# Gated cross-attention layer: rows of x on partitions, probabilities turned by DMA

## The reference, cut to what matters

```python
Sim = (h @ w1)[:, :, None] + (ctx @ w2)[:, None, :] + einsum('bid,bjd->bij', h * w3, ctx) + b_sim[0]   # h = layernorm(x)
A = softmax(Sim, axis=2)
hq_hat = einsum('bij,bjd->bid', A, ctx)
Batt = softmax(max(Sim, axis=2), axis=1)
hc_hat = broadcast(einsum('bi,bid->bd', Batt, h))
x = x + tanh(g_xattn) * (concatenate([h, hq_hat, h * hq_hat, h * hc_hat]) @ W_qv + b_qv)
x = x + tanh(g_ffn) * ffn(layernorm(x))      # router, top 2 of 8 experts, capacity 1280 (not touched)
```

## Time and profile before

| | us |
|---|---|
| three runs, median | 2335.67 |
| lowest and highest of the three | 2333.89, 2336.94 |
| the profiled execution's own time | 2335.5 |
| its span | 2333.8 |
| PE busy | 2220.5 (95%) |
| DVE busy | 1631.7 (70%) |
| ACT busy | 1139.5 (49%) |
| mean granted clock of PE | 0.985 |

### The profile page before, as it was taken

How to read it: one execution, slowest core, us unless ns; L and a number is a source line. 1 busy time by engine, 2 the same in 40 slices (tenths; PEclk the granted TensorE clock), 3 DMA queues, 4 the chain that set the end, 5 groups by cost and what they waited for, 6 DMA issues and landing times.

```text
span 2333.8 us, 46974 instructions
## 1 busy us (share of the span) xinstructions
PE 2220.5 (95%) x16817; PEld 1607.4 (69%) x16817; DVE 1631.7 (70%) x3445; ACT 1139.5 (49%) x1607; POOL 144.6 (6%) x143
## 2 busy tenths in 40 slices
PE   5899999999999999999879998599999999999997
PEld 4788888888888888888634544456564655656463
DVE  7688888888888888887856678546554555646450
ACT  6565555544555554555633334336362534546260
POOL 0000000000000000000002222101101010100101
PEclk9999999999999999999999999799999999999999
DMA  7811110011111001101355553333435333333411
GB/s 211 251 28 47 45 45 27 18 45 45 45 45 45 18 27 45 45 27 43 148 200 199 213 184 119 103 104 86 109 124 135 113 99 103 90 103 90 132 61 22
DMA packets 164944, 212.31 MB, mean 91 GB/s; under 512 B 106148, under 2 KB 106276, under 8 KB 156700
## 3 DMA queue, kind: packets, MB, share of 16 engines
q1 hardware_dynamic: 154012, 191.13, 24.9%
q0 software_dynamic: 10880, 20.52, 4.5%
HBM read 123.66 MB, written 71.52 MB: 84 GB/s over the span
## 4 chain that ended last, share of the span: by engine, by line
PE 75%; DVE 13%; ACT 4%; issue 4%; DMA 1%; DVEq 1%; ACTq 0%; POOL 0%; another core or an unknown queue 0%; SPq 0%; POOLq 0%
PE ps L1275 20%; PE ps L1951 18%; PE ps L1966 18%; PE ps L1288 12%; PE ps L1701 5%; DVE arena L828 1%; DVE arena L727 1%; DVE arena L725 1%; ACT arena L1150 1%; DVE arena L822 1%; DVE arena L750 1%; DVE arena L815 1%; DVE arena L734 1%; ACT arena L1147 1%; DVE arena L1530 0%
## 5 line engine op out<-in xcount | busy, mean ns | idle before, releaser
L1275 PE MATMUL ps<-arena 128*128 128x256 f16 x4800 | 555.8, 274 | 25.1 <-DMA arena<-arena 9.9
L1288 PE MATMUL ps<-arena 128*128 (+1 forms) x4864 | 561.0, 273 | 7.3 <-DVE arena L822 7.3
L1275 PEld LDWEIGHTS ps<-arena 128*128 128x128 f16 x4800 | 470.1, 98 | 89.4 <-issue 16.6
L1288 PEld LDWEIGHTS ps<-arena 128*128 128x128 f16 x4864 | 475.2, 98 | 68.0 <-DVE arena L822 7.0
L1951 PE MATMUL ps<-arena 128*128 128x320 f16 x3072 | 421.0, 300 | 17.7 <-DMA arena<-rows 17.7
L1966 PE MATMUL ps<-arena 128*128 128x512 f16 x1920 | 415.7, 379 | 0.0
L1951 PEld LDWEIGHTS ps<-arena 128*128 128x128 f16 x3072 | 301.5, 98 | 136.9 <-issue 17.7
L1966 PEld LDWEIGHTS ps<-arena 128*128 128x128 f16 x1920 | 187.9, 98 | 225.2
L1137 ACT ACTIVATE arena<-ps,arena (+1 forms) x192 | 148.9, 775 | 282.8 <-PE ps L1275 282.8
L1701 PE MATMUL ps<-arena 128*128 128x512 f16 x1080 | 240.4, 380 | 10.6 <-DMA arena<-feats 10.6
L1875 DVE SCALAR_TENSOR_TENSOR arena<-arena 128x640 f16<-128x640 f32 x128 | 113.0, 883 | 136.1 <-ACT arena L1919 136.1
(11 more groups left out here) (249 smaller groups left out, 1821.7 us busy)
## 6 DMA issues: line engine op xcount, KB each, us to landing
arena<-in_L_ffn_w SPq DMA_DIRECT2D x64, 1024.0 KB, 10.0
arena<-feats SPq DMA_DIRECT2D x16, 1536.0 KB
arena<-in_x SPq DMA_DIRECT2D x32, 512.0 KB, 3.9
feats<-arena SPq DMA_DIRECT2D x16, 1024.0 KB, 3.9
rows<-arena SPq DMA_DIRECT2D x1, 10320.0 KB, 32.0
feats<-arena SPq DMA_DIRECT2D x16, 512.0 KB, 3.5
out<-arena SPq DMA_DIRECT2D x16, 512.0 KB, 2.8
arena<-in_L_xattn_W_qv SPq DMA_DIRECT2D x4, 1024.0 KB, 9.6
```

Source lines behind the costliest of these rows:

```text
L1275: mm = pe.matmul(out, ctxT[:, 2 * t + h, s, k, :], query[:, r, k, :], start=(k == 0 and s + r == 0), stop=(k == KD - 1 and s == 1))
L1288: mm = pe.matmul(acc[k], ctxN[:, 2 * t + h, s, k * P:(k + 1) * P], prob[:, bass.ds(a % 3, 1), r, h, :].rearrange("p o i -> p (o i)"), star ...
```

## The change

Scores now have the rows of x on partitions. The unit of work is 128 rows (`U` = 32 units, two halves of a block), and ctx is taken in 7 chunks (`NC`) of four tiles, 512 columns (`TC`, `CW`), of which the last has 130 columns. The queries are the stationary operand and `ctxT`, laid out with ctx rows on the free axis, is the moving one. A row's maximum is then a reduction along the free axis: it goes into the exponential's bias, and the row sum into its accumulator. The last tile's two rows are ordinary columns. The probabilities come out with rows of x on partitions and are turned for the second product by a DMA transpose for each chunk (`turn_p`), from two staging buffers into one buffer for each chunk. In half i of block b (u = 2b + i), PE does the scores of unit u and the products of unit u-2, chunk by chunk, while ACT and DVE do the softmax of unit u-1.

The queries are formed from rows by DVE and turned by DMA (`turn_q`): those of an odd unit in the first half of SP's body, those of the next block's even unit in its second half. The features are stored as rows, and the merge loads them by one DMA transpose for each block (`load_feats`); its order is changed, and the rows of x have a load of their own (`load_x`). In the prologue tiles 0 to 7 are turned by PE and tiles 8 to 25 by DMA, one transpose for each; group scales come from sums of squares in place of sizes, over four tiles; scores of unit 1 follow those of unit 0 by three chunks. The pooled row is accumulated along partitions and summed by PE once at the end. The table of blank rows is written in pieces through the loop. The core of the diff (functions that go with it are left out where there is "..."):

```diff
--- before.py
+++ after.py
-    def load_block(self, sp, x, feats, b, v):
-        rows = bass.ds(b * 256, 256)
-        sp.dma_start(self.ft[v].rearrange("p f s k i -> p (f s k i)"),
-                     feats[bass.ds(b, 1)].rearrange("o p f c -> (o p) (f c)")).then_inc(self.f_loaded[v], 16)
-        sp.dma_start(self.x2[v], x[rows, :].rearrange("(q p) d -> p q d", p=P)).then_inc(self.x_loaded[v], 16)
+    def load_feats(self, sp, feats, b, v):
+        sp.dma_start_transpose(self.ft[v].rearrange("p f s k i -> p (f s k) i"),
+                               feats[bass.ds(b * 256, 256)].rearrange("i f s d -> i (f s d)"))\
+            .then_inc(self.f_loaded[v], 16)
+
+    def load_x(self, sp, x, b, v):
+        sp.dma_start(self.x2[v], x[bass.ds(b * 256, 256), :].rearrange("(q p) d -> p q d", p=P))\
+            .then_inc(self.x_loaded[v], 16)
...
     IB = 256
     NB = NI // IB
     QT = IB // P
+    U = NI // P
     JT = -(-J // P)
-    NP = JT // 2
     FT = mg.FT
     JR = J - (JT - 1) * P
-    AHEAD = 5
-    BY_PE = 4
-    SLOTS = NP + AHEAD
-    assert JT == 2 * NP
+    TC = 4
+    CW = TC * P
+    NC = -(-J // CW)
+    TILES = [(TC * c, min(TC * c + TC, JT)) for c in range(NC)]
+    COLS = [(CW * c, min(CW * c + CW, J)) for c in range(NC)]
+    NPAIR = JT // 2
+    LAST = NC - 1
+    LAG = 3
+    XR = 4
+    BLANKS = 3
+    BY_PE = list(range(2 * TC))
+    assert TILES[LAST][1] - TILES[LAST][0] == 2 and JT == 2 * NPAIR
...
+    UNIT0 = LAG + 2 * (LAST - LAG) + 1
...
+        def turn_ctx(j):
+            sp.wait_ge(c_lo, j // 2 + 1)
+            sp.dma_start_transpose(ctxT[:, :, j * P:(j + 1) * P], ctxN[:, j].rearrange("p s d -> p (s d)"))\
+                .then_inc(ct_turned[j // TC], 16)
+
+        def turn_q(u, q):
+            sp.wait_ge(row_step, RK * (u + 1))
+            apart(sp, sp_passed)
+            sp.wait_ge(qk_done, UNIT0 if isinstance(u, int) and u == 2 else NC * (u - 1))
+            apart(sp, sp_passed)
+            sp.dma_start_transpose(qT[:, q], qh[:, q].rearrange("p s d -> p (s d)")).then_inc(q_turned[q], 16)
+
+        def turn_p(u, c):
+            sp.wait_ge(p_ready, NC * u + c + 1)
+            apart(sp, sp_passed)
+            if not isinstance(u, int) or u:
+                sp.wait_ge(av_done, NC * (u - 1) + c + 1)
+                apart(sp, sp_passed)
+            if c < LAST:
+                sp.dma_start_transpose(PT[:, c], stage[:, c % 2].rearrange("p s j -> p (s j)"))\
+                    .then_inc(pt_turned[c], 16)
+            else:
+                sp.dma_start_transpose(PTl, stl.rearrange("p n j -> p (n j)")).then_inc(pt_turned[c], 16)
...
+        def body(b, first=False, last=False, norms=True, loads=True, piece=None):
+            u = 2 * b
+            for c in range(NC):
+                turn_p(u - 1, c)
+                if c == 1 and not first and not last:
+                    turn_q(u + 1, 1)
+                if c == 3 and loads:
+                    if not first:
+                        sp.wait_ge(acc_step, 2 * (u - 2))
+                        apart(sp, sp_passed)
+                    load_x(b + 2)
+                if c == 4 and not first:
+                    store_f(u - 3, 1)
+                if c == 5 and norms:
+                    store_e(b + 1)
+            if piece is not None:
+                blank_rows(*piece)
+            for c in range(NC):
+                if not last:
+                    turn_p(u, c)
+                if c == 4:
+                    store_f(u - 2, 0)
+                if c == 5 and norms:
+                    turn_q(u + 2, 0)
...
+        for c in range(2, NC):
+            for j in range(*TILES[c]):
+                if j not in BY_PE:
+                    turn_ctx(j)
...
+        turn_q(2, 0)
+        for c in range(NC):
+            turn_p(0, c)
...
+        sp.wait_ge(qk_done, NC * U)
         mg.load_weights(sp)
+        body(NB, last=True, norms=False, loads=False)
...
+        def low(u, par, c):
+
+            dve.wait_ge(hi_done, NC * u + c + 1)
+            p = slot(par, c)
+            if c < LAST:
+                dve.scalar_tensor_tensor(out=stage[:, c % 2, 1, :], in0=p, scalar=pscale[:, c:c + 1],
+                                         in1=stage[:, c % 2, 0, :], op0=ALU.mult, op1=ALU.subtract)\
+                   .then_inc(p_ready, 1)
...
+        def half(b, i, first=False, last=False, norms=True):
+
+
+            u = 2 * b + i
+            par, old = i, 1 - i
+            ob = b if i else b - 1
+            for c in range(NC):
+                if not last:
+                    chunk_max(NC * u + c, par, c)
+                if not (last and i):
+                    low(u - 1, old, c)
+                if c == 0 and not (last and i):
+                    pool_top(u - 1, ob, old)
+                if c == 1 and not (first and not i):
+                    outputs(u - 3, b - 1 if i else b + XR - 2, old)
+                if c == 2:
+                    if not (first and not i):
+                        output_lows(u - 3, old)
+                    if not (last and i):
+                        pool_rows(u - 1, ob, old)
...
+        def probabilities(u, par, c):
+
+            p = slot(par, c)
+            if c == 0:
+                act.wait_ge(m_step, MK * (u + 1))
+                if not isinstance(u, int) or u >= 2:
+                    act.wait_ge(l_step, 2 * u - 2)
+            act.activation(p, p, ACT.Exp, bias=neg[:, par:par + 1], accum_out=ls[:, par, c:c + 1])\
+               .then_inc(exp_done, 1)
+            if c < LAST:
+                if c >= 2:
+                    act.wait_ge(pt_turned[c - 2], 16 * (u + 1))
+                elif not isinstance(u, int) or u:
+                    act.wait_ge(pt_turned[c + 4], 16 * u)
+            elif not isinstance(u, int) or u:
+                act.wait_ge(pt_turned[c], 16 * u)
+            act.wait_ge(exp_done, NC * u + c + 1)
+            if c < LAST:
+                act.activation(stage[:, c % 2, 0, :], p, ACT.Identity, bias=zero[:, 0:1], scale=pscale[:, c:c + 1])\
+                   .then_inc(hi_done, 1)
...
+        def half(b, i, first=False, last=False, norms=True):
+            u = 2 * b + i
+            par, old = i, 1 - i
+            for c in range(NC):
+                if not last:
+                    scores(NC * u + c, c % 4, par, c, NC * (u - 2) + c + 1)
+                if not (last and i):
+                    probabilities(u - 1, old, c)
+                if c == 1 and not (last and i):
+                    pool_weight(u - 1)
+                if c == 2 and not (first and not i):
+                    output_highs(u - 3, old)
...
+        def scores(bank, q, c):
+            a, z = COLS[c]
+            out = psS[bank][:, 0:z - a]
+            for k in range(KD):
+                for s, r in ((0, 0), (0, 1), (1, 0)):
+                    mm = pe.matmul(out, qT[:, q, s * KD + k, :], ctxT[:, r * KD + k, a:z],
+                                   start=(k == 0 and s + r == 0), stop=(k == KD - 1 and s == 1))
+            mm.then_inc(qk_done, 1)
+
+        def products(u, q, c, first=False):
+
+            pe.wait_ge(pt_turned[c], 16 * (u + 1))
+            if c == 0 and not first:
+                pe.wait_ge(acc_step, 2 * u - 3)
+            a, z = TILES[c]
+            for j in range(a, z):
+                if j == JT - 1:
+                    mm = pe.matmul(psO[q], PTl[:, 2, :], ctxN[:, j, 0, :], start=False, stop=True)
+                    continue
+                for s, r in ((0, 0), (0, 1), (1, 0)):
+                    turned = PT[:, c, s * TC + j - a, :] if c < LAST else PTl[:, s, :]
+                    mm = pe.matmul(psO[q], turned, ctxN[:, j, r, :], start=(j + s + r == 0), stop=False)
+            mm.then_inc(av_done, 1)
+
+        def half(b, i, first=False, last=False):
+            u = 2 * b + i
+            for c in range(NC):
+                if not last:
+                    if c == 0:
+                        pe.wait_ge(q_turned[i], 16 * b)
+                    pe.wait_ge(scores_ready, NC * u + c - 1)
+                    scores(c % 4, i, c)
+                if first and not i and c == LAST:
+                    pe.wait_ge(c_tail, 1)
+                products(u - 2, i, c, first)
...
         with sp.Fori(0, NB // 2 - 1) as n:
             for v in range(2):
+                sp.wait_ge(y_done, QT * (2 * n + v + 1))
+                apart(sp, sp_passed)
+                mg.load_feats(sp, feats, 2 * n + v + 2, v)
                 store(2 * n + v, v, n)
                 sp.wait_ge(y_step, YK * (2 * n + v + 1))
                 apart(sp, sp_passed)
-                sp.wait_ge(y_done, QT * (2 * n + v + 1))
-                mg.load_block(sp, x, feats, 2 * n + v + 2, v)
+                mg.load_x(sp, x, 2 * n + v + 2, v)
```

More of the change, by code:

```diff
@@ L706, in query_rows @@
+            s.wait()
+            s.step(dve.tensor_scalar(ew[:, bass.ds(b * QT, QT)], ewt, 1 / LN_SCALE, bs[:, 0:1], ALU.mult, ALU.add))
+        def query_rows(u, b, q, row, at):
```

(91 more changed lines are left out.)

1150 lines of the change are left out of this document (414 added, 736 removed).

## The result

The changed kernel takes 2383.69 us (median of 4 runs, 2381.66 to 2384.46), the kernel before 2336.31 us (2333.89 to 2337.44) on the same chip. The ratio is 1.0203, 95% interval 1.0185 to 1.0221: slower by 2.0%. The profiled execution has a span of 2382.6 us against 2333.8, and a mean granted clock of 0.967 against 0.985.

The account below looks back on a forecast made before the run. It took PE's streaming to bound the attention half. Loop +36, prologue +5, drain +3 and merge -6 made +38 us on 2335.5 us: 2373 us, range 2325 to 2412.

Parts of the forecast that it names:

- Rival A: Attention loop: PE waits for the queries' transpose in each block, then runs at half clock; 2373 us; chance 0.52.
- B: Attention loop: PE waits for the queries, but the clock stays up; 22 us less, 2351 us; chance 0.14.
- C: Attention loop: queries land in time, nothing waits, the shorter block's full 54 us is kept; 2284 us; chance 0.15.
- D: Merge: a features' transpose takes over 17.1 us and each block waits; at 20 us, 41 more, about 2414; chance 0.11.
- The wait, 4.8 us: Attention loop, block boundary: PE stands still until the next block's queries are turned by DMA, 4.8 us (3.3 to 6.0).
- The half clock, 1.6 us: Attention loop, behind each wait for queries: PE returns at half clock, costing another 1.6 us (1.3 to 2.0, lower end 0).
- a clock that stays up through the gap: Attention loop: sign that would make the prediction wrong; it expected granted clock 0.50 for some 3 us behind each gap.
- The block without waits, 65.2 us: Attention loop: if PE never waited, a block of 256 rows would go from 68.8 to 65.2 us.
- The prologue, +5: Before the attention loop: single-tile transposes and ACT's order put PE's first steady half at about 93 us; +5 us (-7 to +15).
- The drain, +3: Between loop and first merge: weights queued ahead of transposes, pooled weight late, 47 us against 44; +3 us (-5 to +12).
- The merge, -6: Merge and route: features' load issued before the store shortens PE's early wait, steady part unchanged; -6 us (-10 to +3).
- The DMA share of the merge, 0.92: Merge: with features loaded by transposes, the DMA share goes from 0.58 to 0.92 within blocks of 17.1 us.

Follow-up runs that it names:

- 18 filler matmuls: Changed kernel plus 18 matmuls that nothing needs, put on PE ahead of its wait for the queries in each block: 2353.67 us.
- the kernel with the earlier turn: Changed kernel with the transpose of the next block's even queries issued after the probabilities of chunk 4 instead of chunk 5: 2290.72 us.
- The later sums: Changed kernel with PE's prologue sums for the group after next taken behind the present group's scores instead of ahead of them: 2374.07 us.

## Why the prediction was right, and where its terms were off

**Direction and main term.** Forecast 2373 us, slower; measured 2383.69. The span grew by 48.8 us where +38 was forecast; of the 10.8 between them the prologue is 9.7, the loop 1.2 and the drain 1.0, and merge and experts take 1.0 back. Rival A, the wait and the half clock in every block, is what happened. B (clock stays up) falls by the twelve matmuls behind each gap, of which none took less than 4.06 us, and by the 18 filler matmuls, C (queries in time) by 14 gaps, D (features bind the merge) by merge blocks of 17.1 us without idle time. C is however what one moved issue makes of the kernel: it gave 2284, the kernel with the earlier turn 2290.72.

**The wait, 4.8 us.** Measured 4.22. The chain was right link by link. Two errors cancel: DVE's low part began 0.04 us after the high part, not 0.31 (595.88 against 595.03 + 0.81), and the queries' turn came 1.60 behind the probabilities', not 1.33. What is left is 0.3 us by which the high part began sooner (1.99 behind the scores, not 2.29), and PE's own work after chunk 5: 597.55 - 593.04 = 4.5 us to the end of its last matmul, where I had 4.1. Landing took 3.38 us where I had 3.3: 5.35 + 3.38 - 4.51 = 4.22.

**The half clock, 1.6 us.** Measured 2.0: 71.57 - 69.60 by the filler. Wait and clock together came to 71.57 - 65.25 = 6.3 us, against 6.4 forecast. That is close in part by luck: the wait (4.35 us of the block) was forecast too long and the clock loss too short, by 0.4 us each. The Trainium skill ("TensorE: Matmul & The Clock Gate", section "HAM oscillation") says that such a loop starts each turn at half clock. The trace agrees in part: behind 6 of the 14 gaps PE came back at 0.50, behind the other 8 at 1.00, and the clock fell 0.3 to 1.3 us later. I had also named a clock that stays up through the gap as a sign of being wrong. In these 8 it did stay up, and fell behind the gap. So the cost that I gave the clock held, and the picture of a clock that falls in every gap did not.

**The block without waits, 65.2 us.** Measured 65.25 once the wait is away (65.4 with the first block). The whole loop: forecast 1067.6, measured 1068.9.

**The prologue, +5: the term that was off.** Measured +14.7, at the upper bound. I had put the high parts behind the eviction of the scores in ACT's order, which is so. The step that failed is the one after: I closed the chain over the turned tiles, and let the scores of a group run beside ACT's work for the next. But PE itself stood behind the squares, at the sums it takes ahead of the scores. The later sums give 6.0 of the 9.7 us of error back. The scores there also run at half clock (5.28 us for twelve), where I had 2.6.

**The drain, +3.** Measured +4.0, with another split. Instead of 4 us for the weights and 6 for the pooled weight it is one wait of 10.63 us, all from the weights on the queue: once they are spread out 7.0 us are gained, and the pooled weight costs 3.23.

**The merge, -6.** Measured -6.2 for the stage, from -12.7 at its start. I had put the gain at the start down to the new order of the loads; the old order gives back only 4.1 of it. From the third block to the first matmul of the experts it took 1535.42 - 1251.28 = 284.1 us against 1485.78 - 1208.14 = 277.6, so 6.5 us came back, 3.9 of them in longer waits late in the merge (18.6 us in all against 14.7). With the old order of loads the stage took 318.3 us, only 1.5 more, though 4.1 + 4.9 us were lost in waits for features: part of what is won at the start is waited out later. The forecast number held by that balance, which I had not worked out, and the spread of 5 us between kernels with the same merge loop is nearly as large as the term.

**The DMA share of the merge, 0.92.** Measured 0.72. The window of one merge block:

```profile
1281.00:1298.00 17.00, 17.00 (x116) 8.56 (x114) 11.88 (x48) 6.15 (x8) 4.55 (x5) 1.00 0.72 200
```

Line 249 by itself (ns on SP; then issue to landing):

```profile
L249 SPq DMA_TRANSPOSE arena<-feats x16: 6017/6222/13029, 1206.9 to 1467.5; - x16
...
DMA to landing us min/median/max: 8.1/8.3/16.5
```

I had scaled from transposes of 256 KB inside the arena and come to a share of 0.60 for the features. 0.72 less the 0.32 that was there without them is 0.40. Landing in 8.3 us, they are hidden in 17.1. The estimate from the landing of 640 x 1024 elements, 8.5 to 15.5 us, was the better row. By the rate of the Trainium skill ("DMA: Bandwidth & Descriptors", section "Latency and other measured facts") the estimate was 6.0 us; the trace doesn't show the transfer apart from its latency and the traffic beside it.

## What to carry to other kernels

When a kernel's bound engine reads what a DMA turns, look at where the issue stands in the queue's program and not only at how long the transfer takes: here one chunk earlier (5.2 us of the block) was worth 93 us, 3.9% of the kernel. A gap on TensorE can cost more than its length: here 4.2 us in each block brought another 2.0 in clock, and a loop whose work had got 5% shorter came out slower. And a bulk load that nobody needs yet can hold up small transfers behind it on the same queue: spread between them, 4 MB of weights cost the drain 7.0 us less.

## What was not expected of the hardware

Gaps of 2.1 to 2.3 us left the twelve matmuls behind them at 4.0 to 4.5 us in 11 cases of 14 and at 2.76 us in 3, while in the prologue of before one of 2.39 us had cost nothing. Behind 8 of the 14 gaps of some 4.2 us the clock was still at 1.00 when PE came back, and fell to 0.50 while PE was at work (at 1.00 from 673.70 to 674.70, at 0.50 from 675 to 678). The clock at the first matmul behind a gap therefore doesn't tell what the gap costs. And a transpose of 256 KB, 3.1 us to landing in the median, took 13.6 us behind 4 MB of loads on its queue; one of 1.57 MB, 8.3 us in the median, took 16.5.
